# Layer two's attention scores: 64-row tiles of TensorE for even and odd heads

## What is computed

```python
q = (h @ Wq).reshape(bsz, q_len, NH, HD).transpose(0, 2, 1, 3)        # 16 heads of 64
k = (kv @ Wk).reshape(bsz, k_len, NKV, HD).transpose(0, 2, 1, 3)      # 4 heads of 64, 77 keys
q = _apply_rope(q, cos_q, sin_q)
k = _apply_rope(k, cos_k, sin_k)
k = jnp.repeat(k, groups, axis=1)
scores = jnp.einsum('bhqd,bhkd->bhqk', q, k) / math.sqrt(HD)
scores = scores + attention_mask
```

## Time and profile before

| | us |
|---|---|
| median of 3 runs | 2741.8 |
| lowest, highest | 2733.3, 2741.8 |
| the profiled execution | 2738.3 |
| its span, first to last instruction | 2736.5 |
| TensorE busy with streams | 2187.1 (80%) |
| TensorE busy with weight loads (beside streams) | 1578.0 (58%) |
| VectorE | 1833.9 (67%) |
| ScalarE | 1134.4 (41%) |
| GpSimd | 922.2 (34%) |
| mean granted TensorE clock | 0.883 |

### The profile page before, as it was taken

One profiled execution on the slowest core, in us unless ns is written; L12 is line 12 of the kernel. 1 busy time (PEld: TensorE's weight loads), 2 busy tenths in 40 slices (PEclk: granted clock), 3 DMA queues, 4 the chain that ended last, 5 costly groups with the idle time before them and its releaser, 6 DMA issues.

```text
span 2736.5 us, 42481 instructions
## 1 busy us (share of the span) xinstructions
PE 2187.1 (80%) x10536; PEld 1578.0 (58%) x10536; DVE 1833.9 (67%) x3344; ACT 1134.4 (41%) x1891; POOL 922.2 (34%) x1628
## 2 busy tenths in 40 slices
PE   3489668887978788888888788888888887889776
PEld 2233346565756566565656566665656555656665
DVE  1266667678685867678685868677786868686522
ACT  1122444534444354534444444535354444444211
POOL 1111334334243434334242434343342424343212
PEclk8665789999989899999989899999999898989998
DMA  6765545353535344353535354353545353543110
GB/s 142 237 122 123 112 94 109 75 123 77 126 63 116 76 98 108 72 123 79 123 73 123 63 109 95 81 120 78 119 77 116 71 122 59 115 80 81 32 38 5
DMA packets 750939, 263.78 MB, mean 96 GB/s; under 512 B 661884, under 2 KB 735344, under 8 KB 750000
## 3 DMA queue, kind: packets, MB, share of 16 engines
q1 hardware_dynamic: 747439, 262.13, 44.8%
q10 hardware_dynamic: 3328, 0.01, 0.1%
HBM read 97.01 MB, written 26.60 MB: 45 GB/s over the span
## 4 chain that ended last, share of the span: by engine, by line
PE 57%; DVE 13%; issue 13%; ACT 6%; SPq 5%; DMA 2%; POOL 2%; DVEq 1%; ACTq 0%; POOLq 0%
PE work L1346 21%; PE work L1356 14%; PE rowps L1414 7%; PE outps L1401 5%; ACT E L857 5%; PE work L1508 4%; DVE Pn L1009 3%; PE work L1517 2%; PE work L1617 2%; DVE hids L1149 2%; PE work L1339 2%; DVE scaled_row L1002 1%; DMA PT<-Pn 1%; SPq L508 1%; DVE st L1025 1%
## 5 line engine op out<-in xcount | busy, mean ns | idle before, releaser
L1002 DVE TENSOR_SCALAR_CACHE_REDUCE scaled_row<-rowps,der 128x1024 bf16<-128x1024 f32 x512 | 655.2, 1280 | 390.9 <-PE rowps L1414 377.0
L857 ACT ACTIVATE E<-rowps,ebias,der 128x1024 f32<-128x1024 f32 x512 | 615.4, 1203 | 541.1 <-DVE Pn L1009 531.1
L1414 PE MATMUL rowps<-KC,QM 128*128 128x512 bf16 x1024 | 348.7, 428 | 338.7 <-ACT E L857 329.5
L1009 DVE TENSOR_SCALAR Pn<-E,rowinv 128x1024 int16<-128x1024 f32 x512 | 411.5, 804 | 104.7 <-DMA PT<-Pn 59.0
L696 POOL TENSOR_TENSOR rowden<-rowsum,raw 128x1 f32<-128x1 f32 x512 | 126.6, 247 | 979.9 <-ACT E L857 977.8
L1414 PEld LDWEIGHTS rowps<-KC,QM 128*128 128x128 bf16 x1024 | 81.1, 100 | 471.5 <-ACT E L857 364.0
L699 POOL TENSOR_TENSOR rowinv<-rowden,minus 128x1 f32<-128x1 f32 x512 | 300.0, 586 | 92.0 <-POOL rowden L696 91.9
L1401 PE MATMUL outps<-PT,VB 128*16 128x256 f16 x2048 | 304.6, 299 | 0.0
L1401 PEld LDWEIGHTS outps<-PT,VB 128*16 128x16 f16 x2048 | 176.9, 96 | 134.2 <-issue 79.3
L1346 PE MATMUL work<-hTs,ff_w_sb 128*128 128x256 f32 x1024 | 237.5, 383 | 1.2 <-ACT hTs L834 1.2
L1346 PEld LDWEIGHTS work<-hTs,ff_w_sb 128*128 128x128 f32 x1024 | 195.2, 192 | 36.8 <-issue 3.5
(11 more groups left out here) (144 smaller groups left out, 3270.9 us busy)
## 6 DMA issues: line engine op xcount, KB each, us to landing
VW<-vw_dram SPq DMA_DIRECT2D x32, 640.0 KB, 5.1
KC<-k_dram SPq DMA_DIRECT2D x64, 256.0 KB, 2.8
K<-k_dram SPq DMA_DIRECT2D x16, 616.0 KB, 3.9
VB<-v_dram SPq DMA_DIRECT2D x64, 128.0 KB, 2.7
PT<-Pn SPq DMA_TRANSPOSE x512, 3.1
V<-v_dram SPq DMA_DIRECT2D x16, 320.0 KB, 3.7
vw_dram<-scs SPq DMA_DIRECT2D x32, 154.0 KB
K<-k_dram SPq DMA_DIRECT2D x16, 308.0 KB, 3.2
```

What stands on the lines that cost most here:

```text
L857: nc.scalar.activation(E[:, n % 2, :], rowps[n % 2][:], ACT.Exp, bias=ebias[:, n:n + 1], scale=der[:, AL1:AL1 + 1], accum_out=rowsum[:, n: ...
L1002: nc.vector.tensor_scalar(scaled_row[:, n % 2, :], rowps[n % 2][:], der[:, NAL1:NAL1 + 1], 3.0e38, ALU.mult, ALU.min, accum_out=ebias[:, n ...
L1009: nc.vector.tensor_scalar(Pn[:, n % 2, :], E[:, n % 2, :], rowinv[:, n:n + 1], 255.0, ALU.mult, ALU.min).then_inc(row_round.sem, 1)
L1414: ins = nc.tensor.matmul(rowps[n % 2][:, e * (S // 2):(e + 1) * (S // 2)], QM[:, h % 4, t * P:(t + 1) * P], KC[:, h // 4, e * (S // 2):(e ...
```

## The change

The four matmuls of an item are replaced. The even item of a pair now issues nothing; the odd one does the work of both. For each head pair `mm` (now all four of the token tile's half) and each of cosine and sine there are two matmuls: one with partitions 0 to 63 (the even head, 77 key columns) into the even item's bank, one with partitions 64 to 127 (the odd head, 77 key columns) into the odd item's bank. The zeros of `K1` are no longer read, though it is laid out as before. The last matmul into each bank raises `h_filled`. VectorE's write puts the even item's scores in heads 0, 2, 4, 6 and the odd item's in 1, 3, 5, 7. In the planner, the second item of a pair in `sc0`, `sc1` and `sc2` must follow the first at once.

```diff
+PAIRS = ("sc0", "sc1", "sc2")
@@ places
             c = max((c for c in able if able[c] <= soon + 0.1), key=left)
+            for x in ("low", "high"):
+                i = len(at[x])
+                if 0 < i < len(ITEMS[x]) and ITEMS[x][i][0] in PAIRS and (i - item(ITEMS[x], ITEMS[x][i][0])) % 2 == 1:
+                    c = x
             i = len(at[c])
@@ high_dve, scores
-                            out=sc1[:, n % 3, 4 * q:4 * q + 4, :], in0=ps, scalar=HD ** -0.5,
+                            out=sc1[:, n % 3, q::2, :], in0=ps, scalar=HD ** -0.5,
@@ high_pe, sc0 and sc1
-                    for e in range(2):
-                        mm = 2 * q + e
+
+                    if q == 0:
+                        even = ps
+                        continue
+                    for mm in range(4):
                         g = 2 * hf + mm // 2
                         for cs, src in ((0, qc), (1, qs)):
-                            ins = nc.tensor.matmul(ps[:, e * 2 * M:(e + 1) * 2 * M], src[:, mm, t * P:(t + 1) * P],
-                                                   K1[:, cs, g, :], start=(cs == 0), stop=(cs == 1))
-                    ins.then_inc(h_filled.sem, 1)
+                            for pos, bank in ((0, even), (1, ps)):
+                                d = slice(HD * pos, HD * pos + HD)
+                                ins = nc.tensor.matmul(bank[:, mm * M:(mm + 1) * M], src[d, mm, t * P:(t + 1) * P],
+                                                       K1[d, cs, g, pos * M:(pos + 1) * M], start=(cs == 0), stop=(cs == 1))
+                                if mm == 3 and cs == 1:
+                                    ins.then_inc(h_filled.sem, 1)
```

## The result

| | before | changed |
|---|---|---|
| median, us | 2741.8 | 2768.7 |
| lowest, highest | 2733.3, 2744.7 | 2763.0, 2772.7 |
| profiled execution's span | 2736.5 | 2770.9 |
| mean granted clock in it | 0.883 | 0.874 |

The changed kernel takes 1.0103 times as long, with a 95% interval of 1.0079 to 1.0128: 27 us slower. Beside other kernels on a second chip it was 1.0124 [1.0092, 1.0155]. The forecast was 2737 and the range 2726 to 2814 holds the time, but the sign is wrong.

A forecast was written before the change was run, and what follows sets the result against it. No engine is full, so the order of waits decides, the last-ending chain being TensorE's for 57%. Gains of 6.1 us at `sc1` and 0.8 at `sc0`, together 7, by path share 5, gave 2737 us; range 2726 to 2814.

The forecast's parts named there:

- The burst: Score matmuls of a pair on TensorE: both tiles load beside each other, 1.76 us instead of 2.09, 0.33 less.
- Rivals 1: Score bursts: the two tiles' loads pass one after the other, 3.5 us a burst, 2811 us; 0.18, plus 0.05 for the clock.
- Rival 2: Score bursts: instructions taken in order over both tiles, loads beside each other, burst 2.8 us, 2781 us; chance 0.07.
- 3: Score bursts: tiles do not run at once but loads hide, burst 2.11 us, total 2749 us; chance 0.04.
- 4: Score bursts: half-height loads are no bound, burst 1.06 us, total 2714 us; chance 0.06.
- The order of the items and the planner's rule: Planner's rule that a pair's second item follows the first: same 63 items, times and banks, cost nothing.
- The bank's wait: Second burst waits for the first's even-item read: `sc0` loses the first burst's gain; `sc1` 0.10 us at most, absorbed.
- The clock: TensorE falls to 1.2 GHz in the bursts because the array streams 0.066 of each 0.11 us; same price as slow loads; 0.05.
- The change of shape: Switching TensorE's array between tile shapes: 0.09 us each, three changes, 0.28 us for a group of four items.
- the prediction's own sign: Test on TensorE's score bursts: the prediction is wrong if a burst is longer than 2.2 us.
- The even item's wait on VectorE: Even item's fill comes at burst end: hidden at `sc0`; at `sc1` the maxima after the reads end 0.14 us later, no more.
- The share of the path: About 0.7 of the layer-two score matmuls' time is on the path, turning 7 us of gain into 5.

The follow-up runs named there:

- the coupling alone: Changed kernel's joint filling of a pair's two banks in the odd item's place, but with the kernel before's 128-row, 154-column matmuls: 2761.0 us, 1.0086.
- late fill: Kernel before, with the even item's h_filled raised together with the odd item's; matmuls, banks and places as before: 2739.7 us, 1.0008.
- shared banks: Kernel before, with the even item also waiting for the odd item's bank before its matmuls, its fill staying early: 2745.4 us, 1.0027.

## Why the prediction was wrong

**The burst.** The term was right in kind and nearly in size. The loads of the two row tiles run beside each other: 1.95 us from start to the next matmul, of which 1.76 + 0.09 = 1.85 had been put in. Part of that is luck. The prediction read from the earlier trace rows that a tile's instructions are taken up while older ones of the other tile still wait; with 16 in a row they were not (3.57 us). The burst is short because its instructions alternate, and the prediction never named that as a condition. Rivals 1 (its loads), 2, 3 and 4, which wanted bursts of 3.5, 2.8, 2.1 and 1.1, are out for the warm bursts. Rival 2 was also given as what the Trainium skill's rule would make of the burst ("TensorE: Matmul & The Clock Gate", Part 3, The mechanism). That took from it only that matmuls keep their order. The same section lets a load for other rows of the array go ahead of matmuls under way, and in the trace the two tiles' loads do run beside each other (four in 0.30 us); with that, order alone does not give 2.8. The order of the items and the planner's rule changed nothing, as said.

**The bank's wait.** This is the step that failed, together with the clock below. The text had the wait: nothing of the second burst starts before the first burst's even item is read. It put it at 2.38 us after the start at `sc1`, "taken up by the change of shape", and at `sc0` as a lost gain and nothing beyond. In the warm groups that was not far off: at `sc1` the second burst starts 2.58 us after the first (1848.93 to 1851.51) and the group takes 4.52, against 2.20 + 0.43 + 2.09 = 4.72 for a warm group before; 0.20 saved where 0.38 were put in. At the `sc0` shown it starts at 3.24. With the coupling alone and the old matmuls a warm group takes 5.05 us at `sc0` and 4.88 at `sc1` against 4.72; the 28 groups of the steps with self-attention hold 6.9 us more than before (146.7 against 139.8). And it was priced only on one group in a steady unit. The chain of burst, read, burst has no cover in the four groups of the steps without self-attention, where no `rowps` stands between the bursts: 0.74 us of idle TensorE in each of the four, and at the two `sc1` TensorE cold in both bursts and after. I had not looked at these steps. The runs put the coupling at 24 us with the old matmuls, where the sum had a few tenths of a us a group taken from the gain; 16 of them are at `sc1`. Most of it appears only when late fill and shared banks come together (1.0008 and 1.0027 alone).

**The first burst's bank.** The text spoke of the banks between bursts only. The first burst now also needs the odd item's bank, which is that of a `pt` item before: the 0.56 us `<-ACT pTs L946`, at the two last `sc1`. That is 1.1 of the 4.1 us of waits in the four groups (with 4 x 0.74).

**The clock.** It stood in rival 1 with 0.05, as a fall in all bursts. The sum put it at nothing. What happened is between: in the profiled execution 13 of 64 bursts ran wholly at 1.2 GHz, 3.6 us instead of 1.95 (none did before, though first bursts at `sc1` began so; 7 in the other trace of the changed kernel), and some took what followed with them (7.05 us for the 20 matmuls instead of 4.48). The price of the rival, 69 us, was that of all bursts; what the 77 columns cost by measurement is 15.5 us against 128 columns, 8 either way. The row it rested on was right, the chance was too low: the text had itself worked out that the array would stream 0.066 of every 0.11 us. By the prediction's own sign, a burst of over 2.2 us, it was wrong in these bursts.

**The change of shape.** 0.09 for each held roughly for the way out: 1.95 less 16 x 0.112 = 1.79 leaves 0.16 for the burst's first load, which nothing hides, and the way out. The way in can't be read where the bank's wait covers it.

**The even item's wait on VectorE** was put at nothing, and alone it costs nothing that can be told (1.0008). It matters through the bank. **The share of the path** (0.7) has no run that tests it.

**The sum.** Forecast -5 us. In its place, from the runs on one chip, where the changed kernel was 27.7 us slower: 8.6 us of loss in the last steps (15.5 in the two traces), 15.5 for the short streams' clock in the others, and 3.6 that are left with both repaired, in which the gain of about 0.2 us for a warm group at `sc1` is contained. They add to 27.7 because they are differences of the same four medians; each is uncertain by what its two kernels scatter. Two small slips of the prediction change nothing: the median stood 3.5 us above the profiled execution and not 3.4, and a wait that it takes as 0.15 us elsewhere is 0.11 in the 1508.05 at `sc0`.

What stays open: the coupling's trace is 22.8 us longer than the trace before. 10.6 are in the last three stretches and 6.9 in the 28 groups ahead of them, where it is waiting and not the clock (13.0 us at 1.2 GHz in these groups against 15.3). 2.6 stand before the first `sc0`, and the rest, under 3 us, is not placed. Open is too why the last steady step is 2.3 us longer with 128 columns, and how a later or earlier VectorE shifts the wait for the rotated queries ahead of `sc0` (`DVE hids`, 9.2 us in all in the changed kernel's steady steps and 1.3 before), after which the clock fell.

## What to carry to other kernels

When two results are made together, look at both sides of every buffer: a late fill alone cost nothing that can be told here and a shared wait alone 7 us, both together 24, most likely because the next burst then stands behind a read that stands behind this burst. Price a change in every kind of step that runs it, also in the first and last ones where other work no longer covers a wait. And an instruction that becomes bound by its weight load should be asked what the array streams meanwhile: padding 77 columns to 128 cost about 0.1 us in a warm group (4.61 against 4.52 at `sc1`) and gave back 15.5 us, up to 12 of it by the clock.

## What the runs showed of the hardware

Two tiles of 64 rows load weights beside each other: 32 f32 loads of 64 x 128 and their streams in 1.95 us warm, where one tile after the other takes 3.57. In that burst the instructions of the two tiles alternate by two; with 16 of one tile in a row there was nearly no overlap, and nothing between was tried. The Trainium skill says that different tiles can load and multiply in parallel ("TensorEngine Tiling (Array Packing)", Key Properties); the trace agrees for instructions that alternate (1.95 us), and not for 16 in a row (3.57).

The granted clock went with how much the array streams, and not only with whether it has instructions. With 77 columns for each load of 0.11 us the clock stayed at 1.2 GHz through two bursts and beyond (0.57 over 16 us of which PE is busy 14.7); with 128 columns at the same instructions it was up again before the second burst (0.89 over the same stretch, PE busy 13.9). In the steps with self-attention, after about 2 us of idle TensorE, the second burst ran at 1.2 GHz at five of five places with 77 columns and at none of three with 128.
